# Attention and routed mixture on one core: post-attention steps moved between VectorE, ScalarE and GpSimd, and a paired output bank

## The chip, the cores and the metric

The kernel runs on one core of a Trainium2 chip. The time is device microseconds of one execution. Before the change three runs gave 700.45 us as median (699.07 to 701.12). The engines are called as in the profile: PE (TensorE), DVE (VectorE), ACT (ScalarE), POOL (GpSimd), and SP, which issues most DMA transfers. Each engine works through its own instructions in order, and semaphores tie the engines together.

## The reference

One transformer layer on x of 8 sequences x 512 tokens x 128 values, in float32:

```python
x = x + attention(layernorm(x))        # 16 heads of 8 values, softmax over 512 keys,
                                       # times head_mask, then @ Wo.T + bo
y = layernorm(x)
logits = y @ Wr                        # 8 experts
p, i = top_k(softmax(logits), 2); p = p / sum(p)
x = x + gelu(y @ Wfc_s + bfc_s) @ Wproj_s + bproj_s
      + sum over the two chosen experts of p * (gelu(y @ Wfc[e] + bfc[e]) @ Wproj[e] + bproj[e])
```

Each token goes through a shared expert and through two of eight routed experts (hidden size 512).

## The kernel before

The program has four stages.

1. To about 76 us: first layer norm, q, k and v. q and k are split into three bf16 parts, stored in DRAM by SP (`store_parts`) and loaded back in another layout (`load_group`). POOL computes the third parts (`third_parts`, L430).
2. From 76 to about 472 us: attention, sequence by sequence (b = 0 to 7), each in four head groups (hg = 0 to 3) of four heads, each group in 16 steps s. Four steps make a block. A step has one key-score matmul (`key_scores`, L1172, 128 keys x 512 queries), whose exponential ACT takes into `probs` (L676), and on average one row-score matmul (`row_scores`, L1154) for the group after next, whose maxima DVE takes in pairs (`row_max`, L827, eight per group, p = 0 to 7). At the end of each block stand the four matmuls of `pv` (L1183), which add probabilities times v into PSUM bank `BK_O`; they lie eleven steps behind. The key scores use two PSUM banks, so a step waits for the exponential two steps before it. The row scores use four banks, so a pair waits for the maxima of the pair two before it.
3. Inside stage 2 the sequence before (b-1) is finished and routed. All of that uses one PSUM bank, `BK_M`, in turn with the transposed maxima (`max_rows` on PE, L1198, at s = 7 of each head group, copied by ACT, `max_out`, L663). The turns of `BK_M` in one sequence are: output projection of b-1 (`project_out`, L1209, hg = 1), added to x by DVE (`residual`, L858); transposes of the normalised rows (`transpose_y`, L1222, hg = 2), copied by ACT (`copy_yT`, L653); router logits (`router`, L1228, hg = 3); ranks (`ranks`, L1239 to L1246, hg = 3), from which DVE makes the slots. POOL then scatters each sequence's rows to their slots by eight indirect DMAs (`put_rows`, L514), one sequence later. For b = 7 all this stands after the attention.
4. From there to the end: table of tiles, routed experts in 71 tiles, shared expert, and the sum.

The order in each engine is written out by hand: PE's in `attend` by the step s, ACT's in `exps`, DVE's in `attend` by the pair p, POOL's in `gather_and_route`. What decides between engines is which semaphore an instruction waits for. `max_rows` of hg = 2 waits for `s_x2`, the residual of b-1, since it writes the bank that the projection stood in:

```python
if hg == 2:
    wait(pe, s_x2, b)
```

The second layer norm is: four `bn_stats` on DVE (L865), ten small operations on POOL (`ln2_scales`, L472 to L486), then four operations of 256 values on ACT (`ln2_normalise`, L644, after steps -1, 3, 7 and 11 of hg = 2). `out_norm` on DVE turns `BK_O` over in four steps (transpose L835, reciprocal L838, multiplication by head mask and reciprocal L843, and for the last head group a transpose, L850), once per head group.

Of the kernel before, what the change touches and what calls it, by code (L numbers as in the profile page):

```python
# [56 lines left out]
def block_kernel(nc, x, WqT, WkT, WvT, WoT, bq, bk, bv, bo, head_mask, W1, b1, W2, b2, Wr, ident, iota8,  # L57
# [11 lines left out]
    with ctx:  # L69
# [11 lines left out]
        mask_sb = sb("mask_sb", [P, HG])  # L81
# [29 lines left out]
        o_rec = sb("o_rec", [P, S // 32])  # L111
        o_all = sb("o_all", [P, S // 32, HG, D])
        o_sb = sb("o_sb", [P, S])
        logits, top8 = sb("logits", [P, NT, E]), sb("top8", [P, NT, 8])
        top_i = sb("top_i", [P, NT, 8], u32)
# [3 lines left out]
        zero_sb = sb("zero_sb", [P, TH, C])  # L119
        dump_sb = sb("dump_sb", [P, K2 * E, TH, 1], u32)  # L120
        fill_sb = sb("fill_sb", [P, E, TH, ROW])
        tri_f, tri_bf, ones_bf = sb("tri_f", [P, P]), sb("tri_bf", [P, P], bf16), sb("ones_bf", [P, P], bf16)
# [17 lines left out]
        yT_now = xnT[:, 0, :]  # L140
# [32 lines left out]
        s_w1st = sem("first_weights_loaded")  # L173
# [19 lines left out]
        s_keep, s_kept = sem("keep_steps"), sem("yT_kept")  # L193
# [30 lines left out]
        N_W1ST, N_W = 6, 8  # L224
# [10 lines left out]
        PV_LAG, MX_STEP, YT_STEP = 11, 7, 13  # L235
        Y_STEPS = (-1, 3, 7, 11)
        PUT_STEPS = (2, 5, 8, 11, 14, 17, 20, 23)
        ROW_TILES = ((0,), (1, 2), (3,), ())
# [11 lines left out]
        N_PAD = 6  # L250
# [10 lines left out]
        def _(sp):  # L261
# [12 lines left out]
            for j in range(J):  # L274
                m = head_mask.rearrange("(g j) -> j g", j=J)[j, :].partition_broadcast(32)
                with nc.allow_non_contiguous_dma(reason="16 values"):
                    sp.dma_start(mask_sb[32 * j:32 * j + 32, :], m).then_inc(s_w, 16)
# [136 lines left out]
        def _(pool):  # L414
# [37 lines left out]
            nc.gpsimd.memset(v_op[:, :, :, :, 0:1], 1.0).then_inc(s_pad, 1)  # L452
            nc.gpsimd.memset(zero_sb[:, :, :], 0.0).then_inc(s_pad, 1)
# [7 lines left out]
            def gather_v(b, hg):  # L461
                wait(pool, s_pv, NT * (b * HG + hg - HG + 1))
                src = v_all[:, b, :, J * D * hg:J * D * (hg + 1)].rearrange("p n (j d) -> p n j d", j=J)
                nc.gpsimd.tensor_copy(v_op[:, hg, :, :, 1:1 + D], src).then_inc(s_vop, 1)
# [23 lines left out]
            def keep_yT(b):  # L488

                pool.wait_ge(s_yT, b + 1)  # L490
                pool.sem_inc(s_keep, 1)
                nc.gpsimd.tensor_copy(yT[:, b, :], yT_now[:, :]).then_inc(s_kept, 1)
# [14 lines left out]

            def put_rows(b, i, k):
# [11 lines left out]


# [6 lines left out]
            nc.gpsimd.memset(fill_sb[:, :, :, 0:C], 0.0)  # L528
# [7 lines left out]
            def gather_and_route(b):  # L536
                g, last = b * HG, b == B - 1
                max_split(g + 1)
                for n in range(NC):
                    if n == NC // 2:  # L540
                        gather_v(b, 2)
                    if PUT_STEPS[n] > J * NT > PUT_STEPS[n - 1]:
                        max_split(g + 2)
                    if b > 1:
                        route_step(b, n)
# [10 lines left out]
                if b > 0:  # L556
                    keep_yT(b - 1)
# [885 lines left out]
```

## Time and profile before

| | |
|---|---|
| median of three runs | 700.45 us (699.07 to 701.12) |
| profiled execution | 700.0 us, span 698.2 us |
| busy over the span | PE 91%, DVE 77%, ACT 63%, POOL 37% |
| chain that ended last, by engine | PE 63%, DVE 14%, issue 7%, SP 5%, POOL 4%, ACT 4% |
| granted PE clock over the span | 0.975 of full |

Span is the time between the first and the last instruction of the core. The profiled execution took 1.8 us more than its span. Busy shares are means over stages with different limits. "Issue" is time in which nothing that the profile shows was waited for. The ends of matmuls are modelled, so spacing is better read from starts.

### The profile page before, as it was taken

What the parts mean: (1) busy time and instruction counts of PE and PEld (TensorE: products, weight loads), DVE (VectorE), ACT (ScalarE), POOL (GpSimd) and SP (SyncE); (2) the same over time, 40 slices, a digit from 0 to 9 for tenths busy, and PEclk for the clock granted to TensorE, in tenths of its full rate; (3) what the DMA queues carried; (4) which work ended last, traced back from release to release, by engine and by line L of the source; (5) the groups of instructions that cost most, each with busy time, mean ns of one, the idle gap of its engine ahead of it and who ended that gap; (6) DMA issues with size and microseconds to landing.
All of it is one profiled execution on the core that took longest, in us unless ns stands there. A gap on an engine that the chain in (4) does not pass through costs nothing.

```text
span 698.2 us, 13370 instructions
## 1 busy us (share of the span) xinstructions
PE 633.9 (91%) x3934; PEld 324.6 (46%) x3976; DVE 540.3 (77%) x1180; ACT 437.9 (63%) x953; POOL 256.6 (37%) x386
## 2 busy tenths in 40 slices
PE   1766799999999999999999999997979999999996
PEld 1441222323323323323332332323779999998965
DVE  6998778888998998988989989822656666666558
ACT  0881467777687787787787787793425555555541
POOL 6766200020430420421521512506464555454541
PEclk9996799999999999999999999999999999999998
DMA  5399594411311212212221121000112222212174
GB/s 151 93 335 349 126 237 107 115 46 36 92 44 43 83 43 68 69 45 63 63 64 48 58 69 48 21 1 31 47 50 66 66 65 63 68 59 62 47 246 127
DMA packets 67611, 61.28 MB, mean 88 GB/s; under 512 B 16250, under 2 KB 58106, under 8 KB 67562
## 3 DMA queue, kind: packets, MB, share of 16 engines
q1 hardware_dynamic: 63242, 51.79, 26.7%
q0 software_dynamic: 4320, 8.89, 3.8%
q8 instruction: 25, 0.41, 0.3%
q14 instruction: 24, 0.20, 0.1%
HBM read 35.76 MB, written 24.62 MB: 86 GB/s over the span
## 4 chain that ended last, share of the span: by engine, by line
PE 63%; DVE 14%; issue 7%; SPq 5%; POOL 4%; ACT 4%; DMA 3%; DVEq 0%; ACTq 0%; POOLq 0%; another core or an unknown queue 0%
PE ps L1183 13%; PE ps L1172 13%; PE ps L1154 12%; PE ps L1357 10%; PE ps L1369 8%; DVE mx L827 6%; POOL slots L514 2%; DVE x_sb L1097 2%; SPq L295 2%; DMA q_op<-mxT 2%; PE ps L1309 1%; DVE o_t L835 1%; PE ps L1209 1%; PE ps L1317 1%; SPq L305 1%
## 5 line engine op out<-in xcount | busy, mean ns | idle before, releaser
L676 ACT ACTIVATE probs<-ps 128x512 f32<-128x512 f32 x512 | 278.8, 595 | 102.5 <-PE ps L1172 87.8
L827 DVE TENSOR_REDUCE mx<-ps 128x2 f32<-128x1024 f32 x256 | 304.0, 1212 | 42.8 <-PE ps L1154 37.5
L1154 PE MATMUL ps<-k_op,q_op 96*128 96x512 bf16 x512 | 181.5, 394 | 19.2 <-DVE mx L827 7.0
L1172 PE MATMUL ps<-q_op,k_op 128*128 128x512 bf16 x470 | 179.0, 387 | 2.2 <-DMA q_op<-mxT 1.5
L1172 PEld LDWEIGHTS ps<-q_op,k_op 128*128 128x128 bf16 x512 | 49.6, 98 | 187.5 <-ACT probs L676 127.7
L1183 PE MATMUL ps<-probs,v_op 128*32 128x512 f32 x1024 | 136.0, 604 | 0.5 <-issue 0.2
L723 ACT ACTIVATE probs<-ps,b_cur 128x128 f32<-128x128 f32 x284 | 81.4, 368 | 75.7 <-PE ps L1357 65.3
L577 POOL DMA_INDIRECT results<-rest,row_id x71 | 73.9, 1041 | 75.1 <-DVE rest L1041 57.1
L514 POOL DMA_INDIRECT slots<-route_sb,slot_u x64 | 67.0, 1046 | 75.1 <-ACT probs L676 50.8
L1357 PE MATMUL ps<-xn,qk 128*128 128x128 f32 x568 | 79.2, 284 | 3.7 <-DVE xn L1034 1.7
L1154 PEld LDWEIGHTS ps<-k_op,q_op 96*128 96x128 bf16 x512 | 49.5, 99 | 61.7 <-DVE mx L827 27.6
L1369 PE MATMUL ps<-k_op,probs 128*128 128x128 f32 x568 | 75.3, 276 | 0.0
L1357 PEld LDWEIGHTS ps<-xn,qk 128*128 128x128 f32 x568 | 70.1, 195 | 8.7 <-ACT probs L723 8.3
L499 POOL CAST mx_parts<-mx 128x16 bf16<-128x16 f32 x32 | 6.3, 198 | 184.0 <-DVE mx L827 184.0
L1369 PEld LDWEIGHTS ps<-k_op,probs 128*128 128x128 f32 x568 | 69.3, 192 | 0.2 <-issue 0.2
L1041 DVE TENSOR_TENSOR rest<-ps,b_sb 128x128 f32<-128x128 f32 x71 | 20.2, 285 | 23.9 <-PE ps L1369 23.8
L1034 DVE COPY xn<-ps 128x128 f32<-128x128 f32 x71 | 20.6, 291 | 22.1 <-PE ps L1347 12.8
L1183 PEld LDWEIGHTS ps<-probs,v_op 128*32 128x32 f32 x1024 | 20.4, 108 | 34.8 <-issue 31.2
L702 ACT ACTIVATE probs<-ps,b_sb 128x512 f32<-128x512 f32 x32 | 21.1, 689 | 20.9 <-PE ps L1309 18.4
L1317 PEld LDWEIGHTS ps<-w_sb,probs 128*128 128x128 f32 x256 | 29.5, 192 | 2.1 <-issue 1.9
L1025 DVE COPY qk<-w_sb 128x512 f32 x71 | 29.8, 420 | 0.6 <-issue 0.6
L1317 PE MATMUL ps<-w_sb,probs 128*128 128x128 f32 x256 | 29.9, 276 | 0.0
(135 smaller groups left out, 591.8 us busy)
## 6 DMA issues: line engine op xcount, KB each, us to landing
q_op<-q_scr SPq DMA_DIRECT2D x96, 96.0 KB
k_op<-k_scr SPq DMA_DIRECT2D x96, 96.0 KB
w_sb<-in_W SPq DMA_DIRECT2D x18, 256.0 KB, 4.0
probs<-slots SPq DMA_DIRECT2D x71, 64.5 KB, 1.9
k_scr<-probs SPq DMA_DIRECT2D x16, 256.0 KB, 3.7
q_scr<-probs SPq DMA_DIRECT2D x8, 384.0 KB, 3.1
k_scr<-probs SPq DMA_DIRECT2D x8, 384.0 KB, 3.6
k_scr<-probs SPq DMA_DIRECT2D x16, 128.0 KB, 3.1
```

Of the source, the lines that this page charges most:

```text
L514: nc.gpsimd.indirect_dma_start(slots, bass.IndirectOffsetOnAxis(slot_u[:, K2 * i + k:K2 * i + k + 1], 0), y2[:, i, k, :], None).then_inc(s ...
L577: nc.gpsimd.indirect_dma_start(results, bass.IndirectOffsetOnAxis(row_id[:, v, h:h + 1], 0), r_tile[:, v, h, :], None).then_inc(s_res[v], 16)
L676: nc.scalar.activation(probs[:, i, j, :], ps[:, BK_S + j % key_banks(b, hg), :], ACT.Exp, scale=float(D) ** -0.5).then_inc(s_exp, 1)
L723: nc.scalar.activation(hid_tile[:, par, c, :], ps[:, BK_TU + 2 * par + c // 2, TR * (c % 2):TR * (c % 2 + 1)], ACT.Gelu_apprx_tanh, bias=b ...
L827: nc.vector.reduce_max(mx[:, slot % 2, 2 * p:2 * p + 2], ps[:, bank:bank + 2, :], AX.X).then_inc(s_max, 1)
L1025: nc.vector.tensor_copy(w1_cur[:, v, :], w1_sb[:, e, :])
L1154: last = nc.tensor.matmul(ps[:, BK_A + a % 4, :], q_op[hg][0:SH, j, P * i:P * (i + 1)], k_op[hg][0:SH, j, :], start=True, stop=True)
L1172: nc.tensor.matmul(ps[:, BK_S + j % key_banks(b, hg), :], k_op[hg][:, j, P * i:P * (i + 1)], q_op[hg][:, j, :], start=True, stop=True).the ...
L1183: last = nc.tensor.matmul(ps[32 * j:32 * j + 32, BK_O, :], v_op[:, hg, i, j, :], probs[:, i, j, :], start=(i == 0), stop=(i == NT - 1))
L1317: last = nc.tensor.matmul(ps[:, DN0 + b % 2, C * i:C * (i + 1)], hid[:, b % 2, c, P * i:P * (i + 1)], w2_sb[:, E, c, :], start=(c == 0), s ...
L1357: last = nc.tensor.matmul(ps[:, BK_TU + 2 * par + c // 2, TR * (c % 2):TR * (c % 2 + 1)], w1_cur[:, v, P * c:P * (c + 1)], yT_tile[:, par, ...
L1369: last = nc.tensor.matmul(ps[:, BK_TD + par, C * h:C * (h + 1)], hid_tile[:, par, c, P * h:P * (h + 1)], w2_cur[v][:, c, :], start=(c == 0 ...
```

## The change

The edits, most of them in stage 2:

- The head mask is multiplied into the rows of `Wo` once, by POOL. Its four loads become one.
- Head groups of a pair share bank `BK_O`: the odd one's v columns stand 16 columns further, and the bank is accumulated over eight `pv` blocks. `out_norm` runs once per pair, in hg = 2 and in hg = 0 of the next sequence.
- The projection is copied out of `BK_M` by ACT (`copy_projection`, after the exponential of s = 6 of hg = 1). POOL adds the copy to x. `max_rows` of hg = 2 waits for that copy, `s_apc`, no longer for `s_x2`. The projection's four matmuls move from s = 0 to 3 to s = 1 to 4.
- `bn_stats` is split in halves and moves to p = 6 and 7 of hg = 1.
- The second normalisation moves from ACT to POOL (`normalise_y`), in one piece behind `ln2_scales`, for b = 0 to 6. For b = 7 it stays on ACT.
- The transposes move from s = 13 to s = 11 of hg = 2, `copy_yT` from after s = 15 to after s = 13. It writes straight to the array that the shared expert reads; POOL's copy (`keep_yT`, L492) goes.
- Router from s = 1 to s = 0, ranks from s = 14 to s = 13 of hg = 3. ACT copies the logits (after s = 2) and the ranks (after s = 15) out of PSUM.
- DVE keeps the maxima, their indices and `chosen`, in five portions at p = 1 to 5. Difference of logits, counts and slots move to POOL (`count_rows`, `find_slots`), in ten small operations.
- The zeroes for the slots come from `fill_sb`; its memset moves ahead of the third parts of b = 2 to 7, and the setting of ones in `v_op` becomes four memsets.
- For b = 7 the counts and slots stay on DVE.

The change is also described as putting the scores in full-array form. The lines of `row_scores` and `key_scores` are the same in both programs.

```diff
+        projected = rest[:, 0, 0, :]
-        PV_LAG, MX_STEP, YT_STEP = 11, 7, 13
-        Y_STEPS = (-1, 3, 7, 11)
+        MX_STEP, YT_STEP = 7, 11
+        AP_STEP = -10
+        ROUTER_STEP, LOGITS_STEP = 0, 18
+        ROUTER_PAIRS = (1, 2, 3, 4, 5)
+        RANKS_AT, RANKS_STEP = 13, 31
...
-            nc.gpsimd.memset(v_op[:, :, :, :, 0:1], 1.0).then_inc(s_pad, 1)
-            nc.gpsimd.memset(zero_sb[:, :, :], 0.0).then_inc(s_pad, 1)
+            for hg in range(HG):
+                nc.gpsimd.memset(v_op[:, hg, :, :, HALF_OUT * (hg % 2):HALF_OUT * (hg % 2) + 1], 1.0).then_inc(s_pad, 1)
+            nc.gpsimd.memset(fill_sb[:, :, :, 0:C], 0.0).then_inc(s_pad, 1)
...
+            def normalise_y(b):
+                pool.wait_ge(s_scale, b + 1)
+                wait(pool, s_put, b * (16 * NC))
+                wait(pool, s_yTp, b)
+                for i in range(NT):
+                    last = nc.gpsimd.tensor_scalar(y2[:, i, :, 0:C], x_sb[:, e_tile(b, i), :].unsqueeze(1).to_broadcast([P, K2, C]),
+                                                   rstd[:, i:i + 1], neg_shift[:, i:i + 1], ALU.mult, ALU.add)
+                last.then_inc(s_yn, 1)
...
+            def residual(b):
+                pool.wait_ge(s_apc, b + 1)
+                sl = x_sb[:, b * NT:(b + 1) * NT, :]
+                nc.gpsimd.tensor_tensor(sl, sl, projected[:, :].rearrange("p (n c) -> p n c", c=C), ALU.add).then_inc(s_x2, 1)
...
+            def find_slots(b):
+                pool.wait_ge(s_cn, (b + 1) * Q + 1)
+                pool.wait_ge(s_rk, b + 1)
+                nc.gpsimd.tensor_tensor(run_bf[:, :], run_bf[:, :], seq_n[:, :], ALU.add).then_inc(s_cn, 1)
+                pool.wait_ge(s_rkc, b + 1)
+                nc.gpsimd.tensor_tensor(at_f[:, :, :], at_f[:, :, :], chosen[:, :, :], ALU.mult).then_inc(s_at, 1)
...
+                nc.gpsimd.tensor_copy(slot_u[:, :], slot_f[:, :]).then_inc(s_slot, 1)
...
+                    if n == NC - 1 and b > 0:
+                        residual(b - 1)
                     if b > 1:
                         route_step(b, n)
-                if b > 0:
-                    ln2_scales(b - 1)
                 gather_v(b, 3)
                 max_split(g + 3)
                 if b > 0:
+                    ln2_scales(b - 1)
+                    normalise_y(b - 1)
                     y_row_ids(b - 1)
...
+            def copy_projection(b):
+                act.wait_ge(s_ap, b + 1)
+                wait(act, s_x2, b)
+                nc.scalar.activation(projected[:, :], ps[:, BK_M, :], ACT.Copy).then_inc(s_apc, 1)
...
                             step = (hg - 2) * J * NT + i * J + j
-                            if step in Y_STEPS and not first:
-                                ln2_normalise(b - 1, Y_STEPS.index(step))
+                            if step == AP_STEP and not first:
+                                copy_projection(b - 1)
...
                 for j in range(J):
                     last = nc.tensor.matmul(ps[32 * j:32 * j + 32, BK_O, :], v_op[:, hg, i, j, :], probs[:, i, j, :],
-                                            start=(i == 0), stop=(i == NT - 1))
+                                            start=(hg % 2 == 0 and i == 0), stop=(hg % 2 == 1 and i == NT - 1))
...
                 if hg == 2:
-                    wait(pe, s_x2, b)
+                    wait(pe, s_apc, b)
```

How the program's order moves, at three places. The rows are of one engine each; `x15` counts instructions in a row. First ACT, from the copy of the maxima at s = 7 of hg = 0 (`mxT`) into hg = 2. Before:

```order
L663 ACTIVATE mxT<-ps 32x128
L676 ACTIVATE probs<-ps 128x512 x16
L663 ACTIVATE mxT<-ps 32x128
L676 ACTIVATE probs<-ps 128x512 x8
L644 ACTIVATE route_sb<-x_sb,neg_shift,rstd 128x2x128
L676 ACTIVATE probs<-ps 128x512 x4
```

and in the changed program, where `rest` is the copied projection and `v_all` the copied transpose:

```order
L728 ACTIVATE mxT<-ps 32x128
L741 ACTIVATE probs<-ps 128x512 x15
L718 ACTIVATE rest<-ps 128x512
L741 ACTIVATE probs<-ps 128x512
L728 ACTIVATE mxT<-ps 32x128
L741 ACTIVATE probs<-ps 128x512 x16
L728 ACTIVATE mxT<-ps 32x128
L741 ACTIVATE probs<-ps 128x512 x6
L702 ACTIVATE v_all<-ps 128x512
```

A copy of 512 columns now stands between the exponentials of s = 6 and s = 7 of hg = 1, one step ahead of the copy of the maxima. The four normalisations in hg = 2 are gone.

Second PE, in hg = 1 from about s = 3 to the `pv` of the second block (`wo_sb` is the projection, `id_bf` is `max_rows`). Before:

```order
L1172 MATMUL ps<-q_op,k_op 128x512
L1183 MATMUL ps<-probs,v_op 32x512 x4
L1209 MATMUL ps<-wo_sb,o_sb 128x128
L1172 MATMUL ps<-q_op,k_op 128x512
L1154 MATMUL ps<-k_op,q_op 128x512
L1172 MATMUL ps<-q_op,k_op 128x512
L1154 MATMUL ps<-k_op,q_op 128x512 x2
L1172 MATMUL ps<-q_op,k_op 128x512
L1154 MATMUL ps<-k_op,q_op 128x512
L1172 MATMUL ps<-q_op,k_op 128x512
L1198 MATMUL ps<-id_bf,mx_parts 128x128
L1183 MATMUL ps<-probs,v_op 32x512 x4
```

and in the changed program:

```order
L1279 MATMUL ps<-wo_sb,o_sb 128x128
L1241 MATMUL ps<-q_op,k_op 128x512
L1223 MATMUL ps<-k_op,q_op 128x512
L1279 MATMUL ps<-wo_sb,o_sb 128x128
L1241 MATMUL ps<-q_op,k_op 128x512
L1223 MATMUL ps<-k_op,q_op 128x512 x2
L1241 MATMUL ps<-q_op,k_op 128x512
L1223 MATMUL ps<-k_op,q_op 128x512
L1241 MATMUL ps<-q_op,k_op 128x512
L1268 MATMUL ps<-id_bf,mx_parts 128x128
L1253 MATMUL ps<-probs,v_op 32x512 x4
```

The last projection matmul has moved into the second block; `max_rows` stands where it stood, behind the key score of s = 7 and ahead of a `pv`.

Third POOL, at the end of the attention (b = 7), down to the eight scatters of sequence 6. Before:

```order
L464 COPY v_op<-v_all 128x16x8
L499 CAST mx_parts<-mx 128x16
L501 TENSOR_TENSOR mx_parts<-mx,mx_parts 128x16
L506 COPY route_sb<-ids_sb 128x8
L492 COPY v_all<-xnT 128x512
L514 DMA slots<-route_sb,slot_u 34816x129 x8
```

and in the changed program:

```order
L517 COPY route_sb<-ids_sb 128x8
L530 TENSOR_TENSOR sum<-chosen 128x32
L531 TENSOR_TENSOR l_diff<-top 128x4
L533 TENSOR_TENSOR sum<-sum 128x16
L536 TENSOR_TENSOR seq_n<-sum 128x8
L542 TENSOR_TENSOR run_bf<-run_bf,seq_n 128x8
L544 TENSOR_TENSOR at_f<-at_f,chosen 128x64
L546 TENSOR_TENSOR at<-at_f 128x32
L548 TENSOR_TENSOR at<-at 128x16
L550 TENSOR_TENSOR slot_f<-at 128x8
L552 CAST slot_u<-slot_f 128x8
L560 DMA slots<-route_sb,slot_u 34816x129 x8
```

The slots are now made by POOL itself, in a row of small operations ahead of the scatters.

## Rows read from the trace of the kernel before

**Rows 1.** Busy time by stretch: start:end, length, then each engine, clock
```profile
175.70:226.00 50.30, 49.00 (x289) 15.81 (x290) 45.09 (x70) 38.02 (x73) 14.32 (x32) 1.00 0.23 59
```

**Rows 2.** Chain that ended last, attention: start us, us, what
```profile
121.57 0.99 PE ps L1183 x8
124.51 1.00 PE ps L1183 x8
...
142.22 2.08 DVE mx L827 x2
...
192.53 2.08 DVE mx L827 x2
```

**Rows 3.** Timeline of PE, second block of hg = 1: start, us, line
```profile
293.69 0.39 PE L1172 MATMUL ps<-q_op,k_op 128*128 128x512 bf16 x1
293.92 0.22 PE L1198 MATMUL ps<-id_bf,mx_parts 128*128 128x128 bf16 x1
```

**Rows 4.** Timeline of ACT, same block
```profile
292.55 2.17 ACT L676 ACTIVATE probs<-ps 128x512 f32<-128x512 f32 x4 [1.09 <-PE ps L1172]
294.61 0.25 ACT L663 ACTIVATE mxT<-ps 32x128 bf16<-32x128 bf16 x1
```

**Rows 5.** Groups by line and form: count | busy us, mean ns
```profile
L835 DVE STREAM_TRANSPOSE o_t<-ps 128x512 f32<-128x512 f32 x32 | 22.6, 707 | 9.0 <-PE ps L1183 9.0
L525 POOL TENSOR_TENSOR x_sb<-x_sb,bo_sb 128x512 f32 x8 | 9.8, 1261 | 0.0
L858 DVE TENSOR_TENSOR x_sb<-ps,x_sb 128x512 f32<-128x512 f32 x8 | 5.5, 692 | 5.1 <-PE ps L1209 5.1
L492 POOL COPY v_all<-xnT 128x512 f32<-128x512 f32 x8 | 4.9, 612 | 13.2 <-ACT xnT L653 13.2
L653 ACT ACTIVATE xnT<-ps 128x512 f32<-128x512 f32 x8 | 4.8, 602 | 0.7 <-PE ps L1222 0.7
L418 POOL MEMSET q_op<- 128x1024 f32 x4 | 3.8, 950 | 0.0
```

**Rows 6.** Timeline of PE at two waits for DVE, hg = 1 and 3
```profile
298.67 0.38 PE L1154 MATMUL ps<-k_op,q_op 96*128 96x512 bf16 x1
299.29 0.39 PE L1154 MATMUL ps<-k_op,q_op 96*128 96x512 bf16 x1 [0.24 <-DVE mx L827]
...
323.69 0.38 PE L1154 MATMUL ps<-k_op,q_op 96*128 96x512 bf16 x1
324.43 0.39 PE L1154 MATMUL ps<-k_op,q_op 96*128 96x512 bf16 x1 [0.36 <-DVE mx L827]
```

**Rows 7.** Chain that ended last, first stage
```profile
36.29 3.40 POOL probs L430 x3
39.69 1.44 DVE xn L777 x2
```

**Rows 8.** Timeline of DVE, first stage
```profile
33.64 1.45 DVE L777 TENSOR_SCALAR xn<-x_sb,mean,rstd 128x128 f32<-128x128 f32 x4
...
37.42 3.71 DVE L777 TENSOR_SCALAR xn<-x_sb,mean,rstd 128x128 f32<-128x128 f32 x4
```

**Rows 9.** Chain that ended last, behind the attention
```profile
470.95 0.78 issue
471.73 1.09 POOL slots L514
...
481.71 0.21 POOL mean_d L472
...
483.18 0.21 POOL mean_d2q L480
...
483.46 0.21 POOL var_eps L482
...
484.86 0.21 POOL neg_shift L486
```

**Rows 10.** Timeline of ACT, the last six exponentials
```profile
468.60 3.12 ACT L676 ACTIVATE probs<-ps 128x512 f32<-128x512 f32 x6
```

More of the change, by code:

```diff
@@ L273, in _ @@
             sp.dma_start(iota_sb[:, :], iota8).then_inc(s_w, 16)
[L274 to L277, printed above, removed]
+            sp.dma_start(mask_sb[:, :], head_mask.rearrange("(c o) -> c o", o=1)).then_inc(s_w, 16)
             sp.dma_start(wr_sb[:, :], Wr).then_inc(s_w, 16)
@@ L868, in router_step, with ln2_stats @@
-            def router_step(b, step):
-                if step == 0:
-                    dve.wait_ge(s_lgp, b + 1)
-                    nc.vector.tensor_copy(logits[:, :, :], ps[:, BK_M, 0:NT * E].rearrange("p (n e) -> p n e", e=E)).then_inc(s_rt, 1)
-                elif step == 1:
-                    dve.wait_ge(s_rt, b * R + 1)
+            def ln2_stats(b, half):
+                if half == 0:
+                    dve.wait_ge(s_x2, b + 1)
+                    dve.sem_inc(s_bn, 1)
+                for i in range(NT // 2 * half, NT // 2 * (half + 1)):
+                    last = nc.vector.bn_stats(stats[:, i, :], x_sb[:, e_tile(b, i), :])
+                if half == 1:
+                    last.then_inc(s_st, 1)
@@ L875, in router_step, with copy_logits @@
+            def copy_logits(b):
+                dve.wait_ge(s_lgp, b + 1)
+                nc.vector.tensor_copy(logits[:, :, :], ps[:, BK_M, 0:NT * E].rearrange("p (n e) -> p n e", e=E)).then_inc(s_lgc, 1)
+            def router_step(b, step):
+                half = slice(NT // 2 * (step % 2), NT // 2 * (step % 2 + 1))
+                if step < 2:
+                    if step == 0:
+                        dve.wait_ge(s_lgc, b + 1)
+                        wait(dve, s_gd, b)
                     dve.sem_inc(s_bn, 1)
-                    for i in range(NT):
+                    for i in range(half.start, half.stop):
@@ L877, in router_step @@
                         last = nc.vector.max(top8[:, i, :], logits[:, i, :])
                     last.then_inc(s_rt, 1)
-                elif step == 2:
-                    dve.wait_ge(s_rt, b * R + 2)
-                    nc.vector.tensor_tensor(l_diff[:, bass.ds(b * NT, NT)], top8[:, :, 1], top8[:, :, 0], ALU.subtract).then_inc(s_gd, 1)
-                    for i in range(NT):
+                elif step < 4:
+                    dve.wait_ge(s_rt, b * R + step - 1)
+                    for i in range(half.start, half.stop):
```

184 lines of the change are left out of this document (103 added, 81 removed).

## The prediction

> **What bounds the kernel now.** I read busy time by stretch first, then the chain that ended last, then the timelines of PE, ACT and DVE around the moved steps. In a middle sequence PE is busy 49.0 of 50.3 us at the full granted clock (1.00), DVE 45.1, ACT 38.0, POOL 14.3 [rows 1]. The chain goes through PE: an ordinary block of four steps takes 2.94 us (121.57 to 124.51), a sequence 50.31 us (142.22 to 192.53) [rows 2]. Sixteen blocks make 47.1 us, so 3.2 us a sequence are extra: the matmuls of b-1's projection, transposes, router and ranks, and waits. Work taken from ACT or POOL is thus worth nothing in itself. From DVE it is worth what PE waits for DVE. Two such waits stand in each sequence, in hg = 1 and hg = 3, seen where row-score matmuls that else follow each other at 0.22 us start 0.62 and 0.74 us apart [rows 6]: 0.40 and 0.52 us late. Behind the attention POOL leads the chain: eight scatters of sequence 6, from 471.73 to 481.71, then the second layer norm of sequence 7 [rows 9].
>
> I sum against the profiled execution, 700.0 us (span 698.2 and 1.8 around it); it lies 0.45 under the median of the runs shown, and I add that at the end.
>
> **Step 1: DVE's relief.** Per sequence DVE loses two of four transposes of the bank (2 x 0.71), the residual (0.69) [rows 5] and some ten smaller operations: over 4 of 45.1 us. Gone from hg = 1 are residual and transpose, so its wait of 0.40 goes. In its place two halves of the statistics stand at its last two pairs; the second pair then ends some 0.2 us too late for the third row-score matmul of hg = 2. What stays of `out_norm` is twice as wide (reciprocal and multiplication). In hg = 3 the five portions of the router still take up most of DVE's slack. I leave 0.17 of the 0.52 us wait and gain 0.35. Gain of both: 0.14 (counted at the block, where part of the 0.40 is given back) + 0.35, about 0.5. Bounds 0 and 0.9 us.
>
> **Step 2: PE's moved matmuls.** No matmul is added or dropped. The transposes now follow a `pv` instead of standing between key scores, where small waits for exponentials hid part of them: I charge 0.15 us, and 0 for router, ranks and projection together. Steps 1 and 2 give -0.34 a sequence; six full sequences and about half of the last: -2.2 us (bounds +0.5 and -5.5).
>
> **Step 3: a new wait on PE.** This decides. `max_rows` of hg = 2 writes the bank the projection stood in. Before, it waited for a residual that DVE had done long before. Now it waits for ACT's copy, and ACT makes that after the exponential of s = 6, while PE comes to `max_rows` behind the key score of s = 7. In the trace of before that block has four exponentials from 292.55, 0.52 apart ((2.17 - 0.60) / 3), so the third starts near 293.6 and a copy would start at about 294.1; at 0.60 us (ACT's copy of the same 512 columns, [rows 5]) it ends at 294.75 [rows 4]. PE wants `max_rows` at 293.92 [rows 3]. It waits 0.85 us. The last projection matmul, now in this block, pushes both sides by about 0.2 us. Behind `max_rows` in PE's queue stand a `pv` of 1.0 us and all key scores, so nothing fills the gap, and PE is the bound. Seven sequences (b = 1 to 7): 6.0 us. Bounds: 0.5 us each if the copy starts right as its bank is ready (3.5) and 1.1 each if the exponentials bunch up (7.7). The late copy delays one exponential and the maxima's copy by the same amount; the shift rows made from these are wanted only in hg = 2, two blocks (5.9 us) later.
>
> **Step 4: the normalisation on POOL.** In hg = 2 POOL first splits the maxima, then does the ten scale operations (481.71 to 485.07, 3.4 us) [rows 9], then four operations of 256 values. Before has none such. From below a copy of 512 values at 0.61, so 0.31 each; from above the two-input operation of 512 at 1.26 [rows 5]. I take 0.5, near a one-input rate with a fixed part. The last pair of maxima ends some 1.0 us into hg = 2 (half of 2.08 in [rows 2]), and split and statistics add 0.6 (my estimate, three of POOL's small steps of 0.2 in [rows 9]): the normalised values are ready 1.6 + 3.4 + 2.0 = 7.0 us into hg = 2; PE wants them at s = 11, after three blocks, 8.9 us. Free at 0.5, and up to 0.95 each. At 1.26 each they come at 10.0: 1.1 us a sequence. Residual, counts and slots on POOL have slack in the middle sequences, for the scatters that use them are a sequence away. ACT loses four operations and gains three copies; with 38.0 of 50.3 us it isn't the bound.
>
> POOL and DVE get in each other's way in the first stage: four normalisations on DVE took 3.71 us beside POOL's subtractions, 1.45 us otherwise [rows 8]. In the attention the maxima come from PSUM, and I charge nothing; what is exposed is one multiplication a pair. The Trainium skill (GPSIMD Engine Reference, Key points) says that POOL shares its SBUF interfaces with DVE, against DVE operations with two SBUF inputs or in a two-port mode. By that rule the new multiplication could be held by POOL's 256-value operations, up to one of them, and a sequence would lose up to 0.5 us where DVE has no slack left (3.5 us over seven); rows 8 agree with it for another operation, and no row shows it in the attention. I keep zero.
>
> **Step 5: start.** POOL's settings stand right ahead of its subtractions on the chain (36.29) [rows 7]. The memset of 1024 values takes 0.95 us [rows 5] and replaces one of 128; three more small ones come: about 1.0 us later. Behind them the chain goes through the slowed DVE operations, ACT and SP's stores without a gap. Part may be absorbed where ACT is waited for: +0.8 (0 to 1.1).
>
> **Step 6: end of the attention.** The slots of sequence 6 open POOL's chain of ten microseconds, which sets the start of everything behind. Before, DVE made them while the last exponentials ran. Now ACT copies the ranks after its very last exponential (end 468.60 + 3.12 = 471.72 [rows 10]), some 0.2 us as the maxima's copy with its 0.25 [rows 4], and POOL does five dependent operations of 0.28 each (483.18 to 483.46), then the 0.78 us ahead of the first scatter [rows 9]: 471.72 + 0.2 + 1.4 + 0.78 = 474.1 against 471.73, +2.4 us. In the last two head groups, without row scores, the four normalisations gone from ACT and earlier transposes give 0.6 back (0 to 1.5). Net +1.8 (0.8 to 2.6).
>
> **Sum.** -2.2 + 6.0 + 0 + 0.8 + 1.8 = +6.4 us; 700.0 + 6.4 + 0.45 = 706.9 us. With the ends: the least, -5.5 + 3.5 + 0 + 0.8, is 699.3; the most, without step 4, +0.5 + 7.7 + 1.1 + 2.6, is 712.4. They will not all fall on one side, and the forecast's own range is 702.5 to 710.
>
> **Rivals.**
> A. DVE's relief is the larger term and step 3 isn't there. Place: the handing over of the row-score banks. If all PE's waits on DVE go (0.9 a sequence, 5.5 us) and the copy is seldom waited for, since ACT, rid of the normalisations, runs ahead, the time is 700.45 - 5.5 + 0.8 + 1.0 = 696.8. It decides once the new wait is under 0.5 us. For it: DVE's 45.1 of 50.3, and the two waits [rows 1, 6]. Against: ACT can't run ahead of the key scores it reads, and the order fixes one copy between exponential 6 and `max_rows`. 0.12.
> B. Same time: wait and relief cancel, as when the copy costs 0.4 us and relief 0.7: 7 x 0.4 - 4.5 + 0.8 + 1.2, 700.8. 0.11.
> C. The normalisation comes late, as from 0.95 us an operation; at 1.26 each it adds 1.1 x 7 = 7.7: 714.6. Against: one-input copies run at half that. 0.06.
> D. What it is described as doing for the scores isn't done, or does nothing. The lines are alike in both programs, so I give this certainty, and it changes no number.
>
> **Chances.** Forecast 0.71. 0.3% is 2.1 us, about what runs of this kernel can tell from no change. Faster 0.12 (A); same 0.12 (B and the low edge of the forecast); slower 0.76. The range reaches down to 701.5, which leaves out A and half of B, and up to 710.5, which leaves out C.
>
> **What would show it.** PE's timeline in hg = 1 has a gap of about 0.85 us ahead of `max_rows` and names ACT's copy as releaser, seven times, near 6 us in the list of waits. A sequence takes 50.8 us instead of 50.3. PE's waits for DVE fall from two a sequence to small ones. POOL's 256-value operation is near 0.5 us, with no wait ahead of the transposes in sequences 1 to 6. The first scatter of sequence 6 starts over 2 us after the last exponential. The prediction is wrong if there is no gap ahead of `max_rows`, if the sequences shorten by over 0.5 us, or if PE waits for POOL in hg = 2.

## The result, and the profile after

The changed kernel takes 707.0 us as median of four runs (705.9 to 708.1), the one before 700.2 in four runs beside it. The ratio is 1.010, with a 95% interval of 1.0085 to 1.0114. Forecast were 706.9 us. The profiled execution took 708.1 us with a span of 706.2, where before has 700.0 and 698.2.

The busy time of sequence 2, from its first key score to the next sequence's (columns as in [rows 1]: PE with its instructions, weight loads, DVE, ACT, POOL, granted clock, DMA share, GB/s):

```profile
175.40:226.10 50.70, 49.08 (x289) 15.82 (x290) 42.22 (x57) 36.69 (x72) 19.18 (x47) 1.00 0.22 59
```

DVE is relieved by 2.9 us, ACT by 1.3, POOL has 4.9 more, and PE is as busy as before (49.08 for 49.00): of the 0.4 us that the sequence grew by, 0.3 are idle time of PE, the engine that bounds it. Where they stand is seen in PE's timeline of the second block of hg = 1, which answers to [rows 3] (start, length, what, and in brackets the idle time before it with its releaser):

```profile
294.56 0.38 PE L1241 MATMUL ps<-q_op,k_op 128*128 128x512 bf16 x1
295.77 0.22 PE L1268 MATMUL ps<-id_bf,mx_parts 128*128 128x128 bf16 x1 [0.83 <-ACT rest L718]
295.92 1.06 PE L1253 MATMUL ps<-probs,v_op 128*32 128x512 f32 x8
```

L1268 is `max_rows`, which came 0.23 us behind the key score before and comes 1.21 behind it now. ACT in the same block (answers to [rows 4]; L718 copies the projection):

```profile
293.29 1.84 ACT L741 ACTIVATE probs<-ps 128x512 f32<-128x512 f32 x3 [1.09 <-PE ps L1241]
295.03 0.59 ACT L718 ACTIVATE rest<-ps 128x512 f32<-128x512 f32 x1
295.51 0.60 ACT L741 ACTIVATE probs<-ps 128x512 f32<-128x512 f32 x1
296.02 0.27 ACT L728 ACTIVATE mxT<-ps 32x128 bf16<-32x128 bf16 x1
```

The list of waits (sum, times, longest) has it seven times, and one wait for the normalisation on POOL, in the last sequence:

```profile
PE ps L1268 <- ACT rest L718: 5.8, 7, 0.8
...
PE ps L1292 <- POOL route_sb L501: 0.7, 1, 0.7
```

I took the distances of the first key scores of all blocks from the starts of their weight loads (rows PEld), in each trace; some rows of the matmuls themselves are missing. In sequences 1 to 3, 5 and 6 they repeat within 8 ns, so differences of 0.1 us can be read. The table has the means of these five. Sequence 4 is as long as they are before the change (50.31), but in the changed kernel it takes 51.00: its first block has 3.22 us for 2.94, and it has so in every run below.

| us | before | after |
|---|---|---|
| hg = 1, blocks 1 to 4 | 3.78, 3.10, 2.94, 3.26 | 3.78, **4.20**, 2.94, **2.94** |
| hg = 2 | 2.94, 3.00, 2.94, 3.28 | 2.95, 3.00, **3.33**, **3.04** |
| hg = 3 | 3.65, 3.00, 2.94, 3.64 | 3.65, 3.00, 2.94, **3.11** |
| sequence | 50.31 | 50.72 |
| first key score of b = 0 | 76.09 | 76.65 |
| length of b = 0 | 49.34 | 48.02 |
| last key score of b = 7 | 470.06 | 472.12 |
| first scatter of sequence 6 | 471.73 | 476.44 |
| transposes of sequence 7 | 487.33 | 492.03 |
| first scatter of sequence 7 | 497.63 | 505.18 |
| span | 698.2 | 706.2 |

So only 2 of the 8 us are there at the last key score, and 6 arise behind it. There stands POOL (answers to [rows 9]; L544 to L552 make the slots, L560 are scatters, L479 to L493 the scales of sequence 7):

```profile
474.16 0.31 POOL L544 TENSOR_TENSOR at_f<-at_f,chosen 128x64 f32<-128x64 f32 x1 [1.53 <-ACT at_f L712]
...
475.43 0.19 POOL L552 CAST slot_u<-slot_f 128x8 uint32<-128x8 f32 x1
476.44 1.10 POOL L560 DMA_INDIRECT slots<-route_sb,slot_u  x1 [0.83 <-issue]
...
486.41 0.21 POOL L479 TENSOR_TENSOR mean_d<-stats 128x4 f32<-128x4 f32 x1
...
489.56 0.20 POOL L493 TENSOR_TENSOR neg_shift<-neg_mean,rstd 128x4 f32<-128x4 f32 x1
```

and PE behind it (L1292 are the transposes of sequence 7, L1387 is the shared layer's down projection), where the kernel before had 2.10 us of idle time and 3.74 us for the same 32 matmuls:

```profile
492.03 1.11 PE L1292 MATMUL ps<-id_sb,route_sb 128*128 128x128 f32 x4 [4.62 <-ACT route_sb L694]
492.94 6.17 PE L1387 MATMUL ps<-w_sb,probs 128*128 128x128 f32 x32
```

The 6.17 us are the clock. Seven microseconds behind the idle time (the last number but two is the granted clock):

```profile
492.00:499.00 7.00, 6.97 (x38) 6.97 (x38) 0.00 (x0) 2.91 (x5) 0.00 (x0) 0.57 0.01 2
```

A mean of 0.57 is the lower level, 1.2 of 2.4 GHz, for most of the stretch. Before, the shared layer's matmuls of this place ran at 1.00.

The normalisation on POOL went as forecast: 558 ns for an operation of 256 values, over with the last of them 7.0 us into hg = 2 (302.80) and wanted by PE 8.9 us into it:

```profile
307.68 2.17 POOL L501 TENSOR_SCALAR route_sb<-x_sb,rstd,neg_shift 128x256 f32<-128x256 f32 x4
```
```profile
311.69 0.66 PE L1292 MATMUL ps<-id_sb,route_sb 128*128 128x128 f32 x4
```

### The profile page after: what moved, and what is told of

It reads as the page before. It is cut to its first block and busy times, and to the rows that moved or that the text cites. A ratio compares the mean times of both kernels' runs of the same rounds, so it can differ in the third digit from the quotient of the medians.

```text
span 706.2 us, 13367 instructions
## 1 busy us (share of the span) xinstructions
PE 640.1 (91%) x3934; PEld 328.8 (47%) x3976; DVE 523.5 (74%) x1083; ACT 428.4 (61%) x946; POOL 289.8 (41%) x486
## 5 line engine op out<-in xcount | busy, mean ns | idle before, releaser
L560 POOL DMA_INDIRECT slots<-route_sb,slot_u x64 | 66.9, 1045 | 68.2 <-ACT probs L741 42.0
L1387 PEld LDWEIGHTS ps<-w_sb,probs 128*128 128x128 f32 x256 | 32.0, 206 | 2.1 <-issue 1.9
L1387 PE MATMUL ps<-w_sb,probs 128*128 128x128 f32 x256 | 32.3, 289 | 0.0
```

Source lines behind the costliest of these rows:

```text
L560: nc.gpsimd.indirect_dma_start(slots, bass.IndirectOffsetOnAxis(slot_u[:, K2 * i + k:K2 * i + k + 1], 0), y2[:, i, k, :], None).then_inc(s ...
L1387: last = nc.tensor.matmul(ps[:, DN0 + b % 2, C * i:C * (i + 1)], hid[:, b % 2, c, P * i:P * (i + 1)], w2_sb[:, E, c, :], start=(c == 0), s ...
```

## The experiments

Twelve kernels ran, in three groups of four (e1 to e4, e5 to e8, e9 to e12), each group on a chip of its own beside its own runs of the kernel before (medians 700.25, 698.51 and 701.05 us). So ratios are to be compared and not times, and 0.001 is 0.7 us. The changed kernel wasn't run again in these groups: its ratio is that of the section above. Unless said otherwise each is the changed kernel with one edit. The last column is the mean of sequences 1 to 3, 5 and 6.

| run | median us | ratio, 95% interval | sequence us |
|---|---|---|---|
| the change | 707.0 | 1.010, 1.0085 to 1.0114 | 50.72 |
| e1 copy earlier by one step | 702.4 | 1.0023, 1.0009 to 1.0037 | 50.07 |
| e2 projection and copy earlier | 702.0 | 1.0029, 1.0015 to 1.0042 | 50.10 |
| e3 last ranks earlier | 704.6 | 1.0058, 1.0039 to 1.0076 | 50.71 |
| e4 PE kept busy | 705.7 | 1.0078, 1.0053 to 1.0104 | 50.71 |
| e5 copy in an idle place | 696.1 | 0.9971, 0.9958 to 0.9984 | 49.46 |
| e6 clearing late | 705.0 | 1.009, 1.007 to 1.011 | 50.72 |
| e7 residual on DVE | 704.9 | 1.0091, 1.0073 to 1.0108 | 50.71 |
| e8 scatters split | 706.9 | 1.0129, 1.0108 to 1.0149 | 50.72 |
| e9 split, second row buffer | 701.5 | 1.0009, 0.9999 to 1.002 | 50.72 |
| e10 statistics whole | 710.0 | 1.012, 1.0096 to 1.0144 | 51.06 |
| e11 combined | 691.8 | 0.9861, 0.984 to 0.9883 | 49.46 |
| e12 combined, late transposes | 690.1 | 0.9847, 0.9828 to 0.9865 | 49.31 |

### Where ACT's copy of the projection stands (e1, e2, e5)

```
e1: AP_STEP = -10  ->  -11        # copy behind exponential 5 of hg = 1, not 6
e2: AP_STEP = -10  ->  -12        # behind exponential 4
    hg == 1 and s in (1, 2, 3, 4): project_out(b - 1, s - 1)
                       ->  s in (0, 1, 2, 3): project_out(b - 1, s)
e5: AP_STEP = -10  ->  -14        # behind exponential 2
    hg == 1 and s in (0, 1): project_out(b - 1, 2 * s); project_out(b - 1, 2 * s + 1)
```

e1. 

> The changed kernel with ACT's copy of the projection one step earlier, after the exponential of s = 5 of hg = 1; nothing else. Theory (PE waits in max_rows for that copy, 0.83 us, seven times): an exponential is about 0.55 us, so the wait falls to about 0.3 us each, 2 us in the list of waits instead of 5.8, the sequence shortens by about 0.5 us and the kernel by about 3.5 us, to 703.5. Rival (the wait only stands where PE would lose the time anyway, since DVE or ACT set the block): list of waits changes, time stays at 707.

e2. 

> The changed kernel with the projection's four matmuls back at s = 0 to 3 and ACT's copy after s = 4. Theory: the wait is gone altogether, and the second block of hg = 1 returns from 4.20 to about 3.1 us as before the change (0.85 of wait, 0.25 of the projection matmul that had moved there); a sequence takes about 49.6 us instead of 50.7, the kernel 7 to 8 us less, about 699.5. Rival (block bound by DVE or ACT): 707, and another wait in its place. Second rival: the moved matmul costs nothing in itself: 4.20 falls to 3.35 and the first block grows: about 701.

e5. 

> The changed kernel with all four projection matmuls issued behind the first two key scores of the second head group (two behind each) and ScalarE's copy of them behind the third exponential of that group, where ScalarE idles 1.09 us for the next key score. The run with the copy behind s=4 lost 0.49 us a sequence in the second block of this group, and I put that to the copy (0.59 us) and the maxima's copy (0.25 us) falling in one block whose idle time on ScalarE is only about 0.7 us. Theory (the place on ScalarE decides): block 1 keeps about 3.8 us, block 2 falls to 3.0 to 3.1, the sequence to about 49.6 us, the kernel to about 699 (698 to 701). Rival (the copy costs half a microsecond wherever it stands, since it keeps ScalarE from catching up): the sequence stays at 50.1 and the kernel at 702. Second rival: the projections stand too early, TensorE waits in order for the second pair's transposed outputs, and block 1 grows by 0.3 us or more.

One step earlier (e1) takes the second block from 4.20 to 3.55 us and PE's waits for the copy from 5.8 to 1.3 us in all. But two steps earlier, with no wait for the copy left (e2), it stays at 3.59, far from the 3.1 that I expected: the copy pushes the exponentials, and the key score of s = 7 now waits for one. PE, then ACT, in e2, and ACT's next block before the change (it follows [rows 4]):

```profile
293.17 0.39 PE L1241 MATMUL ps<-q_op,k_op 128*128 128x512 bf16 x1 [0.37 <-ACT probs L741]
```
```profile
291.54 0.60 ACT L741 ACTIVATE probs<-ps 128x512 f32<-128x512 f32 x1 [1.09 <-PE ps L1241]
292.04 0.59 ACT L718 ACTIVATE rest<-ps 128x512 f32<-128x512 f32 x1
292.51 1.68 ACT L741 ACTIVATE probs<-ps 128x512 f32<-128x512 f32 x3
294.09 0.25 ACT L728 ACTIVATE mxT<-ps 32x128 bf16<-32x128 bf16 x1
295.03 2.17 ACT L741 ACTIVATE probs<-ps 128x512 f32<-128x512 f32 x4 [0.69 <-PE ps L1241]
```
```profile
295.55 2.16 ACT L676 ACTIVATE probs<-ps 128x512 f32<-128x512 f32 x4 [0.69 <-PE ps L1172]
```

From the start of the copy to that of the next exponential are 0.47 us, and by 0.49 the block is longer than before. ACT's idle time behind the maxima's copy is 0.69 us in both: there it waits for the first key score of the next block, and that one stands on PE behind the key score of s = 7 and the `pv`. So what is put between the exponentials that PE waits for moves everything behind it, and ACT's idle time, 14 us in a sequence, can't take it up. e5 puts the copy in the block before, behind an exponential for which ACT itself had waited, and the second block falls to 3.00 us:

```profile
287.93 0.60 ACT L741 ACTIVATE probs<-ps 128x512 f32<-128x512 f32 x1 [0.50 <-PE ps L1241]
288.42 0.59 ACT L718 ACTIVATE rest<-ps 128x512 f32<-128x512 f32 x1
288.90 0.60 ACT L741 ACTIVATE probs<-ps 128x512 f32<-128x512 f32 x1
289.74 2.17 ACT L741 ACTIVATE probs<-ps 128x512 f32<-128x512 f32 x4 [0.24 <-PE ps L1241]
```

The first block doesn't grow with two projection matmuls behind each of two key scores (3.73 for 3.78), so its length never was theirs. The sequence takes 49.46 us, 1.26 less than in the changed kernel; seven of them are 8.8 us, and the ratios differ by 0.0129, 9.0 us. The theory that the place on ACT decides holds; both rivals fall. These two moves, of the projection and of its copy, make the changed kernel faster than the one before.

### What DVE's relief is worth (e7, e10)

```
e7: POOL's residual(b - 1) dropped; DVE, hg == 1 and p == 5:
    sl = x_sb[:, bass.ds((b - 1) * NT, NT), :]
    nc.vector.tensor_tensor(sl, sl, projected, ALU.add)
e10: hg == 1 and p >= 6: ln2_stats(b - 1, p - 6)
     ->  p == 6: ln2_stats(b - 1, 0); ln2_stats(b - 1, 1)
```

e7. 

> The changed kernel with one piece of the relief undone: the addition of the projection to x runs on VectorE again (from ScalarE's copy, ahead of the statistics in the second head group) instead of GpSimd. It tells what the relief of VectorE is worth there: the last block of this group was 0.316 us shorter a sequence than before. Theory (that block was bound by VectorE's row maxima, and the residual is the piece that delayed them): the block grows from 2.94 back to about 3.2 us, the sequence from 50.72 to about 51.0, the kernel to about 709. Rival (the gain came from the statistics being split into two halves, or from the pairs' common normalisation): nothing changes, 707.

e10. 

> The changed kernel with the statistics of the second normalisation issued in one piece behind the row maxima of the seventh pair in the second head group, instead of in two halves. With the residual put back on VectorE alone, all blocks kept their lengths to 5 ns, so the 0.316 us that the last block of this group gained isn't the residual's. Theory (the normalisation of each head group, which stood in the same half of the group, has gone to the pairs, and that is the relief): the block stays at 2.94 us and the sequence at 50.72. Rival (the split of the statistics matters): the block grows by 0.2 to 0.4 us, the sequence to about 51.0, the kernel by 1.5 to 2.5 us.

e7 refutes my theory for the changed kernel: no block of the middle sequences changes by more than 5 ns. It doesn't put things back as they were, though. The residual stood at p = 1 before and stands at p = 5 here, and behind PE's stall DVE has two idle times of 1.72 and 1.5 us in this group. In e10 the last block of hg = 1 stays at 2.94 us, as the theory of the pairs' normalisation says, but the sequence grows by 0.34 us all the same, as the rival says: it is the first block of hg = 2 that grows, to 3.29. The four statistics together hold up a pair of maxima, and the row scores wait. DVE, then PE, in e10:

```profile
304.22 0.86 DVE L934 BATCH_NORM_STATS2 stats<-x_sb 128x6 f32<-128x128 f32 x4
305.00 3.47 DVE L896 TENSOR_REDUCE mx<-ps 128x2 f32<-128x1024 f32 x3
```
```profile
306.27 0.39 PE L1224 MATMUL ps<-k_op,q_op 96*128 96x512 bf16 x1 [0.28 <-DVE mx L896]
```

So 0.4 us more of work in one place cost 0.34 us, and 0.7 us in another (the residual) cost nothing. Which piece of the relief is worth the 0.32 us of the last block of hg = 1 stays open. PE's stall isn't it, for in e5 there is no stall and the block has 2.94 us too. What is left is that the transpose of the bank and all four statistics stood together between two pairs of maxima, ahead of the row score that waited (DVE before the change; L835 is the transpose, L865 the statistics):

```profile
295.42 0.71 DVE L835 STREAM_TRANSPOSE o_t<-ps 128x512 f32<-128x512 f32 x1
296.05 0.83 DVE L865 BATCH_NORM_STATS2 stats<-x_sb 128x6 f32<-128x128 f32 x4
296.79 1.21 DVE L827 TENSOR_REDUCE mx<-ps 128x2 f32<-128x1024 f32 x1
```

The transpose went and the statistics moved to p = 6 and 7; no run puts either back by itself, and e10 shows that the statistics alone can hold PE up.

### The start (e6)

```
zero_sb = fill_sb[:, 0, :, 0:C]  ->  zero_sb = sb("zero_sb", [P, TH, C])
memset(fill_sb[:, :, :, 0:C])    ->  memset(zero_sb), and the clearing of fill_sb
                                     behind the bias addition
```

e6. 

> The changed kernel with one thing put back at the start: a small zero buffer of its own is cleared early, and the 0.95 us clearing of the filling rows stands again behind the bias addition, far from the first maxima. My step 5 put +0.8 us to this clearing standing ahead of GpSimd's first gathers; the first key score of the attention came 0.55 us later than before. Theory (the clearing is the delay): it comes 0.5 us earlier, at 76.1 us, and the time falls by about 0.5 us to 706.5. Rival (the delay comes from elsewhere in the start, such as VectorE's normalisation, whose instructions lengthened from 715 to 796 ns beside GpSimd): the first key score stays at 76.6 us and the time at 707. This also tells whether sequence 0, which is 1.33 us shorter in the changed kernel, is shorter because its start is later: then it grows back to about 48.6 us.

The first key score comes at 76.34 us. One trace says little, but ten traces with the clearing early have it from 76.65 to 77.67, 77.07 on average, and the three with it late (e6, e11, e12) at 76.34, 76.56 and 76.26, 76.38 on average. The clearing costs 0.7 us of the start, as the theory says; the kernel's time of e6 alone (1.009 for 1.010) doesn't resolve it. Sequence 0 stays at 48.08 us, so its 1.3 us aren't an effect of a late start.

### The end of the attention (e3, e4, e8, e9)

```
e3: ranks in the last sequence at s = 9, not 13; their copy after step 27, not 31
e4: four more 128x512 matmuls on PE between the up projections and the transposes
    of sequence 7, into a bank that nobody reads
e8: for n in range(NC):                     # scatters of sequence 6
        if n == 5: ln2_scales(B - 1)
        put_rows(B - 2, n // K2, n % K2)
e9: as e8 with n == 4, and the rows of b = B - 1 in a buffer y3 of their own,
    without the waits of ACT and POOL for the scatters of sequence 6; DVE's slots of
    sequence 7 wait for them
```

e3. 

> The changed kernel with ranks at s = 9 and the copy of the ranks after s = 11 of hg = 3 in the last sequence alone. Theory (the slots of sequence 6 open POOL's chain behind the attention; they come 2.6 us later against the last key score than before the change): the first scatter starts some 4 us earlier, at about 472.4 instead of 476.4. Everything behind moves with it, and PE's idle time of 4.6 us ahead of the last transposes shrinks, so that its clock isn't halved behind it (another 2.9 us): 700 to 703. Rival (something else is as late, such as the second layer norm's input, the projection of sequence 7): first scatter earlier, but the transposes move by under 1 us: 706.

e4. 

> The changed kernel with four extra matmuls of 128x512 f32 (results unused, in the free output bank) between the shared expert's second up projection and the last transposes, where PE is idle for 4.6 us. Theory (the idle time is what lowers PE's granted clock at 491 us, and the half clock costs 2.9 us in transposes and down projection): the granted clock stays at 1.00 there, the down projection takes 3.6 us instead of 6.0, the profile ends about 2.9 us earlier, 704. Rival (the clock falls whatever PE does there): same, 707.

e8. 

> The changed kernel with one reordering at the end: GpSimd works out the scales of the last sequence's normalisation behind five of the eight scatters of the sequence before, instead of behind all eight. In the changed kernel the eight scatters begin 4.7 us later than before, at 476.4, and the scales wait for them until 486.4 although the statistics are there at about 481. Theory (the late scatters carry through to the end only because the scales are queued behind them): the scales come about 3.8 us earlier, TensorE's idle time ahead of the transposes falls from 4.6 to about 1 us, so its clock doesn't halve there, and the kernel gains 4 to 6 us: 701 to 703. Rival (the scatters themselves are awaited, since the row buffer and the ids of the last sequence are written only when all eight have landed): the last sequence's rows stand still until then and less than 1 us is gained, 706 to 707.

e9. 

> The changed kernel with the last sequence's normalised rows in a buffer of their own, so that ScalarE need not wait until the eight scatters of the sequence before have landed, and the scales worked out behind four of these scatters. With the scales moved alone (behind five), they came at 485.8 us, but ScalarE then waited for the last scatter's landing until 491.1 us and the transposes moved from 492.0 to 493.2: the rival of that run held. Theory (late scatters act through two doors, the queue of GpSimd and the row buffer, and only both open give the time back): scales at about 485, transposes at about 487.5 right behind the up projections, no idle time of TensorE ahead of them, the clock not halved behind them; 4.6 us of idle and 2 us or more of slow matmuls go, so the kernel is at about 1.001 of the one before (0.998 to 1.004), that is 699 to 702 where the one before has 700. Rival (the scatters' queue or its traffic delays something else, as the slots of the last sequence): less than 2 us is gained, a ratio of 1.007 or more.

e3 gains 2.9 us (0.0042), short of the 4 to 7 that the theory gave, though its cause is right: the first scatter comes at 474.65, only 1.8 us earlier and not 4. Four steps are no more in this place, where a block of four without row scores takes 1.97 us; ACT's copy of the ranks stands at 472.02, behind four exponentials fewer. Its transposes come at 490.27, and the clock is low behind them for a shorter time (4.89 us for 6.17).

e4 takes the idle time ahead of the transposes from 4.62 to 1.00 us, and they and the down projection run at full clock. The granted clock in the same stretch as above, 1.00 for 0.57:

```profile
492.00:499.00 7.00, 6.16 (x47) 5.54 (x48) 0.92 (x11) 3.83 (x8) 0.00 (x0) 1.00 0.01 2
```

It gains some 1.5 us, half of what I expected; the intervals overlap, so the size is uncertain in the medians. The profiles give it: the first scatter of sequence 7 starts 30.26 us behind the last key score for 33.06, 2.8 us earlier. What follows varies by itself: from this scatter to the end the changed kernel takes 201.03 us and e6, which is alike there, 199.21. The chain still starts at the same late scales; only the slow matmuls go.

e8 is no better than the changed kernel (the intervals just overlap). The scales come early, at 485.61, and nothing follows from it:

```profile
485.61 0.20 POOL L493 TENSOR_TENSOR neg_shift<-neg_mean,rstd 128x4 f32<-128x4 f32 x1
...
491.06 0.19 POOL L517 COPY route_sb<-ids_sb 128x8 uint32<-128x8 uint32 x1 [1.48 <-DMA slots<-route_sb,slot_u]
```
```profile
491.11 2.07 ACT L695 ACTIVATE route_sb<-x_sb,neg_shift,rstd 128x256 f32<-128x256 f32 x4 [7.49 <-DMA slots<-route_sb,slot_u]
```

ACT may write the rows of sequence 7 into the shared buffer only when the last scatter of sequence 6 has read it, and that scatter now comes later, by 3.2 us, since the scales were put ahead of it. The rival that I had written beside my theory was right. e9 takes both waits away:

```profile
486.59 2.07 ACT L699 ACTIVATE y<-x_sb,neg_shift,rstd 128x256 f32<-128x256 f32 x4 [0.19 <-POOL neg_shift L497]
```
```profile
488.72 0.66 PE L1298 MATMUL ps<-id_sb,y 128*128 128x128 f32 x4
489.21 3.74 PE L1393 MATMUL ps<-w_sb,probs 128*128 128x128 f32 x32
```

No idle time is shown ahead of the transposes and no half clock behind them, and 0.0091 is gained, 6.4 us. With the copy that stalls `max_rows` still in its place the kernel is level with the one before.

### The gains together (e11, e12)

```
e11: e5 + e6 + e3 + e9
e12: e11, and YT_STEP 11 -> 13 (transposes of the normalised rows)
```

e11. 

> All that the runs pointed to in one kernel: the projection behind the first two key scores and its copy behind the third exponential (sequence 49.46 us), the filling rows cleared late, in the last sequence the ranks four steps earlier and their copy behind the twelfth exponential, and the last sequence's rows in a buffer of their own with the scales behind four scatters. Theory (the gains add): the last key score at about 463.5, first scatter 466, scales 475.5, transposes right behind the up projections at 477.5 instead of 483.7 in the run with the early copy, the clock whole there: 6.1 us of idle and about 1.8 us of slow matmuls less than that run, so about 0.986 of the kernel before (0.983 to 0.991), some 689 us. Rival (the end is bound elsewhere, by the shared layer on TensorE and the table on VectorE, which don't move with the transposes): not below 0.993.

e12. 

> The combined kernel with the transposes of the second normalisation two key scores later, as in the kernel before the change. Theory (two key scores later they fall into the wait that stood there, as the kernel before shows): blocks 3 and 4 of the third head group take 0.15 us less a sequence, 1.0 us in seven, 688 where the combined one has 689; a difference in the profile's block lengths, hardly one in the medians. Rival: the copy of these transposes on ScalarE and the router behind it come late and the first block of the fourth head group grows by as much; no difference.

e11 came out as the sum said: 0.9861 for 0.986, with the last key score at 463.13 (463.5), the first scatter at 465.50 (466) and the last of the scales at 476.1 (475.5). The transposes come right behind the up projections as expected, at 478.59 (477.5). PE goes through the place without a gap:

```profile
470.82 7.80 PE L1387 MATMUL ps<-v_all,w_sb 128*128 128x512 f32 x16
478.59 0.66 PE L1299 MATMUL ps<-id_sb,y 128*128 128x128 f32 x4
479.08 3.74 PE L1395 MATMUL ps<-w_sb,probs 128*128 128x128 f32 x32
```

In e12 the last two blocks of hg = 2 take 2.94 and 3.28 us, as before the change, and the sequence 49.31: the moved transposes cost the 0.15 us that step 2 charged, and the theory holds in the block lengths. Its median is 1.7 us lower than e11's for 1.0 expected, and the intervals overlap, so the medians don't show it. It has the lowest time measured, 1.5% faster than before and 2.5% than the changed one.

## Why the prediction was right, point by point

- **Step 3, the new wait.** Right in place, cause and size: 0.83 us for 0.85, seven times, 5.8 us for 6.0. Missed was the price of the fourth projection matmul, which moved out of a block that had room into this one. I had said that it pushes both sides by 0.2 us and didn't put it in the sum. The block grew by 1.11 us, 7.8 us in all, and 0.28 of it stand beside the wait. e1 agrees, with 0.19 us of wait left and a block 0.46 longer than before. That these 0.28 are the matmul isn't shown by a run that moves it alone. Nor did I see that the copy had a second price under the first: without the wait for it, the 0.5 us by which it pushes the exponentials are next (e2), and the right place gives back 1.26 us a sequence (e5).
- **Step 1, DVE's relief.** The mechanism was right, the term too small: 0.32 + 0.54 = 0.85 us a sequence for 0.5. I had charged 0.2 us for the statistics' halves at the end of hg = 1 and left 0.17 of the wait in hg = 3. Neither came. Which piece brought the 0.32 is open. The fear had a ground: issued whole, the statistics cost 0.34 us (e10).
- **Step 2, moved matmuls.** +0.147 us for the transposes, forecast 0.15; e12 takes exactly this back. Ranks and router cost nothing, as said.
- **Step 4, normalisation on POOL.** 558 ns for 0.5, ready at 7.0 us and wanted at 8.9, as worked out; free but for 0.7 us once, in the last sequence with its shorter blocks, where PE had waited 1.05 us for ACT's before. The possible loss through the shared SBUF interface (Trainium skill, GPSIMD Engine Reference, Key points) doesn't show in the attention: in the five sequences of the table no block grew but those of steps 2 and 3, and the new multiplication on DVE took 410 ns. In the first stage the normalisations of L846, the same line as L777 before, take 796 ns on average for 715, which agrees with it but doesn't prove it.
- **Step 5, start.** +0.8 forecast; 0.55 in the two profiles, and 0.7 between the ten traces with the clearing early and the three with it late. What I hadn't seen is that sequence 0 gets 1.3 us shorter. Before, PE waited in it for two loads of shifted rows; now for none.
- **Step 6, end.** The first scatter comes 2.65 us later against the last key score (2.4 forecast, of which I took 0.6 off; the last two head groups gave 0.5 back). What failed is the step's end: I let the delay pass through to the end of the kernel at its own size. At the first scatter of sequence 7 it has grown to 5.5 us: the idle time of PE ahead of the transposes went from 2.1 to 4.6 us and the clock then halved, which cost the transposes 0.45 us and the down projection 2.43.

So the time was met to 0.1 us partly by luck: the attention came out 2 us better than the sum (last key score +2.06 for about +4) and the end worse by as much in the median, 3.5 in the profiled execution, which was one of the slower. The attention's 2 us are themselves a sum of misses: the relief 2.2 us larger and sequence 0 1.3 us shorter than in the sum, the block of step 3 1.7 us longer. (A small slip besides: sixteen blocks of 2.94 us make 47.0, not 47.1; nothing rests on it.) The three rivals fell: PE's wait was there (A), wait and relief didn't cancel (B), the normalisation wasn't late (C). e5 comes near rival A's time: its 0.9971 is 698.4 us on the scale of A's 696.8. But it gets there by a change of the order, and A held that none is needed.

## What to carry to other kernels

An engine's idle time over a long stretch doesn't say that a new operation is free on it. Look for the block in which it lands, ask whether it stands there ahead of something that the bounding engine waits for, and put it where the engine already waits for its input. Where work on a shared buffer is late, list all that the buffer's next writer waits for, the queue and the transfer's landing both, before moving one of them: e8 moved one and gained nothing, e9 both and gained 6.4 us. And a delay ahead of the bounding engine costs more than itself when the idle time makes its clock fall.

## What the runs showed of the hardware

The granted clock behind idle time of PE, at one place of the program, by the time of the 32 matmuls of the down projection (3.74 us at full clock):

| idle before the transposes, us | run | down projection, us |
|---|---|---|
| none shown | e9, e11 | 3.74 |
| 0.69 | e12 | 3.74 |
| 1.00 | e4 | 3.74 |
| 2.10 | before | 3.74 |
| 4.14 | e3 | 4.89 |
| 4.41 | e10 | 5.36 |
| 4.55, 4.58, 4.62, 4.64 | e1, e6, the change, e2 | 6.22, 6.20, 6.17, 6.16 |
| 5.11 | e7 | 5.97 |
| 6.11 | e5 | 5.42 |
| 7.42 | e8 | 5.34 |

In this place the clock stayed at 2.4 GHz in all runs with up to 2.1 us of idle time; in all with 4.1 us or more it was at 1.2 GHz for a part of the matmuls behind it, and the loss (1.2 to 2.5 us) doesn't grow with the idle time. No limit between the two can be read off: behind the 2.55 us of idle time ahead of the last output projection both occur, its eight matmuls take 2.04 or 2.05 us (the change, e1, e2, e6, e7, e9, e11), 1.71 (e4) or 1.13 (e3, e5, e8, e10, e12), and before the change they took 1.91 behind 2.39 us, at a granted clock of 0.54. The Trainium skill (TensorE: Matmul & The Clock Gate, Part 1) says the same in kind: an idle array is throttled to half the rate and its own activity releases it. The trace agrees: the clock is at 0.57 in the stretch behind the idle time and at 1.00 in e4, where PE had work.

## What stays open

Why the loads of shifted rows are no longer waited for in sequence 0 (1.3 us): in the changed kernel and all twelve others this sequence is 1.0 to 1.7 us shorter than in the one trace of before, and at most 0.3 us of such a wait is left (e1, e9, e11), but none undid the part that could bring it. Why the first sequence's start varies by 1 us between kernels with the same first stage. What the first block of sequence 4 loses 0.28 us to. And which piece of DVE's relief is the 0.32 us of hg = 1.
